# A last chunk finished tile by tile, and four smaller moves in a fused attention and mixture-of-experts kernel

## The chip, the cores and the metric

The kernel runs on one core of one Trainium2 chip. The metric is the time of the whole program on that core in microseconds (us): the median of three runs, 1008.57 us before the change (1008.33 to 1008.92). Lower is better.

## The reference, cut to what matters

x has 4096 rows of 128 values. Eight layers of linear attention with a feed-forward block come first; then a mixture of four experts, of which each row uses the two with the highest router weight. Every step ends in a layer norm.

```
x = _layernorm(x + attn(x))                       # 8 layers: q, k, v; elu; K*v and K summed over rows; Wo, gelu;
                                                  # layer norm; Wf1, gelu, Wf2, gelu; layer norm
h_norm = layer_norm(x, rn_g, rn_b)
g = softmax(h_norm @ router_w.T);  top2_w, top2_idx = top_k(g, 2);  top2_w /= sum(top2_w) + 1e-8
hid = relu(layer_norm(x @ w1[e], ln_g, ln_b));    expert_out[e] = hid @ w2[e]
out = layer_norm(sum of top2_w * expert_out over the two, on_g, on_b)
result = _layernorm(x + out)                      # its own mean and variance, no scale
```

## The kernel before

The kernel is written by hand in five instruction streams, one for each engine: `block.sync` (SyncE, the DMA queue), `block.scalar` (ScalarE), `block.tensor` (TensorE), `block.vector` (VectorE) and `block.gpsimd` (GpSimd). In each stream the order is the order of the calls, and semaphores (`wait_ge`, `then_inc`) tie the streams together. Nothing reorders the work: an instruction that waits holds up all that stands behind it on its engine.

**The layers.** Rows come in 32 units of 128 x 128 halves (`u`, `h`; 512 columns to a half), and `run(step)` walks 33 steps in which one unit is projected (`project`), another attends (`attend`) and a third goes through its feed-forward block (`hidden`, `feed_out`), each some 24 us. Products in the `F32R` format come in three parts, high by high, high by low and low by high (`product`, L823 to L825), so weights and inputs are split into a high and a low half first. `first_step` of the tensor stream begins with `fill(44, mean_r)`: 44 products of constants into the bank `O[1]` (L830), which nobody reads. Then come the first products K, V and Q. Their inputs are `wqkv_l` (L1273) and `xr_l` (L1292) of VectorE, which then adds 1 to the parameters (L1669) and begins on K with `min_k` (L1298), `make_k` (L1305) and `k_by_v` (L1314); ScalarE gives it exponentials (`exp_k`, L465). GpSimd splits inputs 4 and 5 (`low_first`, L1944) and after that, in its steps 0 to 3, the weights of the next layer in four pieces (`split_weights`, L1953, L1956, L1963, L1966). In steps 0 to 2 it waits for nothing but the loaded weights and its own earlier pieces; from step 3 on each piece waits for `xl_done[1]`.

**The experts.** The rows are now worked in 8 chunks of 512 rows, 4 tiles of 128 to a chunk. `run_moe(step)` makes 8 steps; a step (it, k) does three things at once: it begins chunk k+1 (`enters`) and routes chunk k (`routes`), it takes chunk k-1 through the experts (`mixes`), and it ends chunk k-2 (`ends`: both layer norms and the store). The last step, (2, 4), only mixes chunk 8 and ends chunk 7; what remains of chunk 8 stands behind it. Within a step:

- TensorE makes eight expert products (`expert_hidden`, L1047 to L1056) into three banks `R`, with the gram products of the next chunk between them (`gram`, L1085 to L1087, all into the bank `O[0]`), from which VectorE takes the variances (`squares`, L1511). ScalarE empties each `R` bank (`relu`, L584).
- `route` (L1066, L1067) multiplies the chunk by the router's weights, into `O[0]` as well, and so waits for all 16 `squares`. VectorE makes the gates from it (`gates`: 20 small operations from L1548 on, with ScalarE's exponential L623 among them) and splits the standard deviations (`split_std`, L1522 to L1528); TensorE turns these (`turn_std`, L1009, into the bank `SV`) and ScalarE copies them out (`rows_of_std`, L553).
- `expert_out` (L1099) makes the output of one tile, 8 products over the 8 parts of `hid`, into `O[1]` (in the trace Ob) or `CB[0]` (Ca) in turn; `mix_tile` (L1627, L1631) on VectorE adds the four experts by their gates. The order on TensorE is `expert_out` 0, `turn_std`, `expert_out` 1, 2, 3.
- The end of a chunk: `stats_mix` (L1443 to L1463) on VectorE, a power on GpSimd (L2049), `negate_mean` (L1646), `norm_mix` on ScalarE (L594), scale and residual on GpSimd (`scale_and_add`, L2061, L2064, with `add_on_b`, L2070, for the residual), `stats_sum`, the power again, `norm_sum` on ScalarE (L604), and one store.

Behind the last step chunk 8 is ended in two pairs of tiles: `last_moments` (L1879 to L1896) on VectorE, `last_root_of` on ScalarE (a logarithm L808 and an exponential L811), `last_scaled` (L1907, L1913), the same once more for the second norm, and `last_result` (L1922), with one store to a pair (L447).

## Time and profile before

| | |
|---|---|
| median of three runs | 1008.57 us (1008.33 to 1008.92) |
| the profiled execution | 1008.5 us, of which the span from first to last instruction is 1006.7 us |
| TensorE matmul, busy | 954.6 us (95%) |
| VectorE, busy | 888.4 us (88%) |
| ScalarE, busy | 825.6 us (82%) |
| GpSimd, busy | 99.2 us (10%) |
| the layers | 0 to about 824 us |
| one chunk of the experts in the steady part | about 22.35 us |
| the last step and what is behind it | 975.3 to 1006.7 us |

In a row of the timeline the first number is the start in us from the span's beginning, the second the time in us that the row covers; then come the engine (PE is TensorE, PEld its weight loads, DVE VectorE, ACT ScalarE, POOL GpSimd, SPq the DMA queue of SyncE), the line, the operation, what is written and read, and the count. In brackets stand the idle time of the engine just ahead and what ended it. Numbers of buffers are left out, so that `R` is any of three banks. Operations of one engine overlap in the records, so that the distance between two starts tells what one costs the queue.

### The profile page before, as it was taken

The numbers are of one execution on the slowest core, as the hardware profiler recorded it, in microseconds if no ns is written. First come the engines' busy times: TensorE is split into PE (matmuls) and PEld (weight loads), VectorE is DVE, ScalarE is ACT, GpSimd is POOL, SyncE is SP. The second block draws the span as 40 slices with busy tenths as digits, with TensorE's granted clock in tenths as the row PEclk, the third lists the DMA queues.
The fourth block names the chain that finished last, engine by engine and source line by source line (L and its number), as shares of the span: only waits on it lengthen the run. The fifth ranks groups of instructions, "written<-read, shape, count | busy, mean of one in ns | idle before, by whom it ended". The sixth has DMA issues, their size and how long they took to land.

```text
span 1006.7 us, 13398 instructions
## 1 busy us (share of the span) xinstructions
PE 954.6 (95%) x3604; PEld 607.4 (60%) x3604; DVE 888.4 (88%) x2338; ACT 825.6 (82%) x1341; POOL 99.2 (10%) x103
## 2 busy tenths in 40 slices
PE   8799999999999999999999999999999889999984
PEld 7455555555555555565555555555555567777773
DVE  6879999999999999999999999999998788888875
ACT  5889999999999999999899999999998854444442
POOL 2000000000000000000000000000001112333331
PEclk9999999999999999999999999999999999999997
DMA  9000000000000000020000000000001000000000
GB/s 342 1 1 0 1 1 1 0 1 1 0 1 1 1 0 1 1 85 0 1 1 7 0 1 1 1 0 1 1 0 62 23 1 1 11 11 12 12 21 21
DMA packets 8200, 15.86 MB, mean 16 GB/s; under 512 B 960, under 2 KB 5440, under 8 KB 8000
## 3 DMA queue, kind: packets, MB, share of 16 engines
q1 hardware_dynamic: 7696, 14.82, 4.2%
q8 instruction: 31, 0.51, 0.2%
q14 instruction: 41, 0.34, 0.1%
q10 hardware_dynamic: 432, 0.20, 0.1%
HBM read 12.92 MB, written 2.10 MB: 15 GB/s over the span
## 4 chain that ended last, share of the span: by engine, by line
PE 64%; ACT 15%; DVE 10%; issue 10%; POOL 1%; POOLq 0%; DVEq 0%; ACTq 0%
PE Oa L929 11%; PE Ob L929 7%; PE R L823 7%; PE R L825 6%; PE R L824 6%; PE SV L970 4%; ACT L668 4%; PE Ob L884 3%; ACT rs L510 2%; ACT L712 2%; ACT rz L489 2%; PE Ca L949 1%; PE Ca L948 1%; PE Cb L884 1%; PE SV L967 1%
## 5 line engine op out<-in xcount | busy, mean ns | idle before, releaser
L529 ACT ACTIVATE hid<-R,par 128x512 f32<-128x512 f32 x224 | 148.6, 698 | 14.2 <-PE R L825 12.2
L929 PE MATMUL Oa<-hid,wraw 128*128 128x512 f32 x256 | 134.6, 607 | 2.6 <-ACT hid L529 1.1
L929 PE MATMUL Ob<-hid,wraw 128*128 128x512 f32 x256 | 130.8, 592 | 0.0
L823 PE MATMUL R<-x_h,wf_h 128*128 128x512 f32 x224 | 106.1, 474 | 0.5 <-ACT hid L529 0.5
L510 ACT ACTIVATE rs<-SV,eps_ln 128x512 f32<-128x512 f32 x128 | 88.3, 690 | 10.1 <-PE SV L970 5.1
L1358 DVE SCALAR_TENSOR_TENSOR y<-x,par,y 128x512 f32<-128x512 f32 x120 | 87.4, 747 | 3.4 <-ACT y L538 3.1
L823 PE MATMUL R<-xr_h,wqkv_h 128*128 128x512 f32 x156 | 86.8, 556 | 2.5 <-DVE Kt L1314 1.1
L1369 DVE TENSOR_TENSOR y_l<-y,y_h 128x512 fp32r<-128x512 f32 x128 | 87.8, 686 | 1.2
L824 PE MATMUL R<-x_l,wf_h 128*128 128x512 f32 x224 | 88.0, 393 | 0.0
L825 PE MATMUL R<-x_h,wf_l 128*128 128x512 f32 x224 | 87.9, 392 | 0.0
L515 ACT ACTIVATE rs<-rs 128x512 f32<-128x512 f32 x128 | 80.7, 631 | 1.2
L929 PEld LDWEIGHTS Oa<-hid,wraw 128*128 128x128 f32 x256 | 45.9, 189 | 36.4 <-ACT hid L529 27.9
L823 PEld LDWEIGHTS R<-x_h,wf_h 128*128 128x128 f32 x224 | 42.1, 188 | 41.8 <-issue 35.9
L970 PE MATMUL SV<-y,mean_all 128*128 128x512 f32 x128 | 65.6, 594 | 1.6 <-ACT rs L510 0.9
L1345 DVE SCALAR_TENSOR_TENSOR V<-Q,kv,rz 128x512 f32<-128x512 f32 x64 | 46.6, 748 | 23.1 <-ACT rz L494 23.1
L929 PEld LDWEIGHTS Ob<-hid,wraw 128*128 128x128 f32 x256 | 48.2, 189 | 24.5 <-issue 16.3
L1365 DVE CAST y_h<-y 128x512 fp32r<-128x512 f32 x128 | 54.4, 425 | 8.9 <-PE R L949 6.7
L825 PE MATMUL R<-xr_h,wqkv_l 128*128 128x512 f32 x156 | 62.0, 398 | 0.0
L824 PE MATMUL R<-xr_l,wqkv_h 128*128 128x512 f32 x156 | 62.0, 397 | 0.0
L499 ACT ACTIVATE y<-Ca 128x512 f32<-128x512 f32 x65 | 38.7, 595 | 25.2 <-PE Ca L949 25.2
L1314 DVE SCALAR_TENSOR_TENSOR Kt<-R,par,Kt 128x512 f32<-128x512 f32 x62 | 46.3, 746 | 10.9 <-PE R L825 10.5
L604 ACT ACTIVATE reluq<-V,rz 128x128 f32<-128x128 f32 x28 | 11.5, 483 | 52.7 <-DVE rz L1646 44.4
(274 smaller groups left out, 2413.4 us busy)
## 6 DMA issues: line engine op xcount, KB each, us to landing
wraw<-w_dram SPq DMA_DIRECT2D x7, 768.0 KB, 11.9
x<-x_dram SPq DMA_DIRECT2D x8, 256.0 KB, 6.0
Q<-x_dram SPq DMA_DIRECT2D x1, 2048.0 KB, 7.8
out_dram<-reluq SPq DMA_DIRECT2D x7, 256.0 KB, 2.3
wraw<-w_dram SPq DMA_DIRECT2D x2, 512.0 KB, 5.5
wraw<-w_dram SPq DMA_DIRECT2D x1, 576.0 KB, 6.4
wraw<-row_dram SPq DMA_DIRECT2D x1, 512.0 KB, 5.1
wraw<-bias_dram SPq DMA_DIRECT2D x1, 512.0 KB, 6.5
```

The costliest lines, as they stand in the source:

```text
L510: nc.scalar.activation(rs[:, half(h)], SV[:, :], ACT.Ln, bias=eps_ln[:, :]).then_inc(ln_done[which], 1)
L515: nc.scalar.activation(rs[:, half(h)], rs[:, half(h)], ACT.Exp, scale=-0.5).then_inc(rs_done[which], 1)
L529: nc.scalar.activation(hid[:, m * CH:(m + 1) * CH], HIDDEN[m][:, :], GELU, bias=param(u // 4, BF1 + m % FB)).then_inc(hid_done, 1)
L823: nc.tensor.matmul(bank, w_h, a_h, start=True, stop=False)
L824: nc.tensor.matmul(bank, w_h, a_l, start=False, stop=False)
L825: return nc.tensor.matmul(bank, w_l, a_h, start=False, stop=True)
L929: mm = nc.tensor.matmul(O[h][:, :], raw(u // 4, WF2 + j * P, P), hid[:, m * CH:(m + 1) * CH], start=(j == 0), stop=(j == FB - 1))
L970: mm = nc.tensor.matmul(SV[:, :], mean_all[:, :], y[which][:, half(h)], start=True, stop=True)
L1345: nc.vector.scalar_tensor_tensor(out=V[:, half(h)], in0=Q[:, chunk(u, h)], scalar=kv[:, b:b + 1], in1=rz[:, half(h)], op0=ALU.mult, op1=AL ...
L1358: nc.vector.scalar_tensor_tensor(out=g, in0=t, scalar=b, in1=g, op0=ALU.add, op1=ALU.add).then_inc(y_done[which], 1)
L1365: nc.vector.tensor_copy(y_h[:, half(h)], y[which][:, half(h)]).then_inc(yh_done[which], 1)
L1369: nc.vector.tensor_tensor(y_l[:, half(h)], y[which][:, half(h)], y_h[:, half(h)].bitcast(F32), ALU.subtract).then_inc(yl_done[which], 1)
```

## The change

1. **The last chunk by tiles.** Each tile of chunk 8 is ended by itself. The last addition of `mix_tile` also gives the sum of the row (`accum_out`), `end_centre` makes the mean from it, ScalarE's `end_rstd_of` takes the square of the centred tile with its row sum, a logarithm and an exponential, and `end_scaled` does scale and residual, again with a row sum for the second norm. `end_result` is stored tile by tile. The steps of tile t stand between those of tile t+1's mixing.
2. **The chunk ahead of it on VectorE and ScalarE.** Chunk 7 is ended without GpSimd: `chunk7_rstd` on ScalarE takes the place of the powers, `chunk7_scaled` and `chunk7_result` on VectorE that of `norm_mix`, `scale_and_add` and `norm_sum`. VectorE does it ahead of the mixing of chunk 8. ScalarE's `norm_sum` of chunk 6 is moved out of the end of step (2, 3) to between the `relu` of the last step.
3. **Banks in the last step.** Output tile 2 of chunk 8 goes into `O[0]`, and tile 3 into four banks, one for each expert (`last_tile_out`), so that TensorE no longer waits for the mixing; `expert_out` of tile 0 waits for each part of `hid` by itself.
4. **The router in another bank.** From chunk 3 on `route` writes `SV` in place of `O[0]` and waits for no `squares`; `turn_std`, which writes `SV` too, waits for the first gate step.
5. **Deviations turned later.** `turn_std` stands behind `expert_out` of tile 1.
6. **Fewer unread products**: 22 in place of 44. And GpSimd's pieces 0 to 2 of the second layer's weights wait for `xh_done[0]` of steps 1 to 3.

```diff
...
+        def router_bank(n):
+            return O[0] if n <= 2 else L[0]
...
         def mixed_bank(n, t):
+            if (n, t) == (CHUNKS, 2):
+                return O[0]
             return R[2] if n == 1 and t % 2 else MIXED[t % 2]
+        def last_bank(e):
+            return (C, L[0], R[0], R[1])[e]
...
+            sp.wait_ge(chunk7_step, 3 * TILES)
+            sp.dma_start(out[:, (CHUNKS - 2) * TILES:(CHUNKS - 1) * TILES, :],
+                         mix[:, half(0)].rearrange("p (t d) -> p t d", t=TILES)).then_inc(out_stored, 16)
+            for t in range(TILES):
+                sp.wait_ge(end_step[t], 5)
+                sp.dma_start(out[:, (CHUNKS - 1) * TILES + t, :], mix[:, par_tile(1, t)]).then_inc(out_stored, 16)
+            sp.wait_ge(out_stored, 16 * (CHUNKS - 1 + TILES))
...
-                    if ends and m == 4:
+                    if ends and m == 4 and not final:
+                    if final and 2 <= m < 6:
+                        norm_sum_tile(it, 1, m - 2)
+                    if final and m == 2:
+                        chunk7_rstd(MIX)
+                    if final and m == 7:
+                        chunk7_rstd(SUM)
...
-                if ends:
+                if ends and it < 2:
                     norm_sum(it, k - 2)
+            def chunk7_rstd(which):
+                act.wait_ge(var_eps_done[which], CHUNKS - 1)
+                nc.scalar.activation(var_eps[which], var_eps[which], ACT.Ln).then_inc(chunk7_root, 1)
+                act.wait_ge(chunk7_root, 2 * which - 1)
+                nc.scalar.activation(rstd[which], var_eps[which], ACT.Exp, scale=-0.5).then_inc(chunk7_root, 1)
+            def end_rstd_of(t, n):
+                col = slice(t, t + 1)
+                act.wait_ge(end_step[t], (1, 4)[n])
+                nc.scalar.activation(unused[:, tile(t)], mix[:, par_tile(1, t)], ACT.Square,
+                                     bias=end_mean[n][:, col], accum_out=end_var[n][:, col]).then_inc(end_root[t], 1)
+                act.wait_ge(end_root[t], 3 * n + 1)
+                nc.scalar.activation(end_var[n][:, col], end_var[n][:, col], ACT.Ln, bias=moe_eps[:, :],
+                                     scale=1.0 / P).then_inc(end_root[t], 1)
+                act.wait_ge(end_root[t], 3 * n + 2)
+                nc.scalar.activation(end_rstd[n][:, col], end_var[n][:, col], ACT.Exp,
+                                     scale=-0.5).then_inc(end_root[t], 1)
             run_moe(step)
+            act.wait_ge(square_done, CHUNKS * TE)
+            for t in range(TILES):
+                end_rstd_of(t, 0)
+                if t > 0:
+                    end_rstd_of(t - 1, 1)
+            end_rstd_of(TILES - 1, 1)
...
-                elif n == 3:
-                    pe.wait_ge(ln_done[1], 2 * UNITS)
+                else:
+                    pe.wait_ge(gate_step, (n - 1) * GATE_STEPS + 1)
...
-                pe.wait_ge(square_done, 2 * EXPERTS if n == 1 else n * TE)
+                if n <= 2:
+                    pe.wait_ge(square_done, (2, 2 * TILES)[n - 1] * EXPERTS)
+                else:
+                    pe.wait_ge(std_rows_done, n - 1)
+                    if n == 3:
+                        pe.wait_ge(ln_done[1], 2 * UNITS)
-                    both = O[0][:, 2 * t * EXPERTS:2 * (t + 1) * EXPERTS]
+                    both = router_bank(n)[:, 2 * t * EXPERTS:2 * (t + 1) * EXPERTS]
...
-                pe.wait_ge(relu_done, n * HB)
+                if (n, t) != (CHUNKS, 0):
+                    pe.wait_ge(relu_done, n * HB)
...
-                after(pe, mix_done, ((n - 1) * TILES + t - 1) * EXPERTS)
+                if (n, t) == (CHUNKS, 2):
+                    pe.wait_ge(square_done, CHUNKS * TE)
+                    pe.wait_ge(gate_step, (CHUNKS - 1) * GATE_STEPS + 1)
+                else:
+                    after(pe, mix_done, ((n - 1) * TILES + t - 1) * EXPERTS)
                 for m in range(HB):
+                    if (n, t) == (CHUNKS, 0):
+                        pe.wait_ge(relu_done, (n - 1) * HB + m + 1)
                     mm = nc.tensor.matmul(mixed_bank(n, t)[:, tile(m // 2)], hid[:, tile(t, m * CH)], w2[:, tile(m)],
...
+            def last_tile_out():
+                for m in range(HB):
+                    mm = nc.tensor.matmul(last_bank(m // 2)[:, tile(0)], hid[:, tile(TILES - 1, m * CH)], w2[:, tile(m)],
+                                          start=(m % 2 == 0), stop=(m % 2 == 1))
+                    if m % 2 == 1:
+                        mm.then_inc(last_out_mm, 1)
...
-                fill(44, mean_r[:, :])
+                fill(22, mean_r[:, :])
...
                     expert_out(it, k - 1, 0)
+                if mixes:
+                    expert_out(it, k - 1, 1)
                 if routes:
                     turn_std(it, k)
                 if mixes:
-                    expert_out(it, k - 1, 1)
                     expert_out(it, k - 1, 2)
-                    expert_out(it, k - 1, 3)
+                    if (it, k) == (2, 4):
+                        last_tile_out()
+                    else:
+                        expert_out(it, k - 1, 3)
...
+                        total = None
+                        if n == CHUNKS and e == EXPERTS - 1:
+                            total = end_sum[0][:, t:t + 1]
                         nc.vector.scalar_tensor_tensor(out=o, in0=mixed_bank(n, t)[:, tile(e)], scalar=gate[:, c:c + 1],
-                                                       in1=o, op0=ALU.mult, op1=ALU.add).then_inc(mix_done, 1)
+                                                       in1=o, op0=ALU.mult, op1=ALU.add,
+                                                       accum_out=total).then_inc(mix_done, 1)
...
+            def end_centre(t, n):
+                if n == 0:
+                    dve.wait_ge(mix_done, ((CHUNKS - 1) * TILES + t + 1) * EXPERTS)
                 else:
...
+                    dve.wait_ge(end_step[t], 3)
+                nc.vector.tensor_scalar(end_mean[n][:, t:t + 1], end_sum[n][:, t:t + 1], -1.0 / P, None,
+                                        ALU.mult).then_inc(end_step[t], 1)
+            def end_scaled(t):
+                yield
+                o = mix[:, par_tile(1, t)]
+                dve.wait_ge(end_root[t], 1)
+                nc.vector.scalar_tensor_tensor(out=o, in0=o, scalar=end_mean[0][:, t:t + 1], in1=on_g,
+                                               op0=ALU.add, op1=ALU.mult).then_inc(end_step[t], 1)
+                yield
+                dve.wait_ge(end_step[t], 2)
+                dve.wait_ge(end_root[t], 3)
+                nc.vector.scalar_tensor_tensor(out=o, in0=o, scalar=end_rstd[0][:, t:t + 1],
+                                               in1=xb[:, par_tile(1, t)], op0=ALU.mult, op1=ALU.add,
+                                               accum_out=end_sum[1][:, t:t + 1]).then_inc(end_step[t], 1)
+                yield
+                end_centre(t, 1)
+            def end_result(t):
+                o = mix[:, par_tile(1, t)]
+                dve.wait_ge(end_root[t], 6)
+                nc.vector.tensor_scalar(o, o, end_mean[1][:, t:t + 1], end_rstd[1][:, t:t + 1], ALU.add,
+                                        ALU.mult).then_inc(end_step[t], 1)
...
+            def chunk7_scaled():
+                dve.wait_ge(chunk7_root, 2)
...
+            def chunk7_result():
+                dve.wait_ge(chunk7_root, 4)
...
+            def last_step():
+                weave(stats_mix(2, 2))
+                chunk7_scaled()
+                weave(statistics(SUM, 2, 2, mix[:, half(0)]))
+                chunk7_result()
+                weave(mix_tile(2, 3, 0))
+                end_centre(0, 0)
+                weave(mix_tile(2, 3, 1), end_scaled(0))
+                end_centre(1, 0)
+                weave(mix_tile(2, 3, 2), end_scaled(1))
+                end_centre(2, 0)
+                weave(last_tile_mixed(), end_scaled(2))
+                end_centre(3, 0)
+                end_result(0)
+                weave(end_scaled(3))
+                end_result(1)
+                end_result(2)
+                end_result(3)
...
-                if 3 <= s < UNITS - 1:
+                if s < 3:
+                    pool.wait_ge(xh_done[0], upto(s, 0))
+                elif s < UNITS - 1:
```

How the order of TensorE stands around the router, before and with the change (chunk 8's routing; `rw_parts` is the router's weights, `consts` by `wraw` the turning of the deviations, `wraw` by `hid` an output tile):

```order
L1066 MATMUL Oa<-rw_parts,x_h 128x8 [waits square_done,xe_l_done]
L1067 MATMUL Oa<-rw_parts,x_l 128x4
...
L1099 MATMUL Ob<-wraw,hid 128x128 [waits mix_done,relu_done]
L1099 MATMUL Ob<-wraw,hid 128x128 x7
L1009 MATMUL SV<-consts,wraw 36x128 [waits std_rows_done,std_split]
L1009 MATMUL SV<-consts,wraw 36x128 x3
L1099 MATMUL Ca<-wraw,hid 128x128 [waits mix_done,relu_done]
L1099 MATMUL Ca<-wraw,hid 128x128 x7
L1099 MATMUL Ob<-wraw,hid 128x128 [waits mix_done,relu_done]
```

```order
L1108 MATMUL SV<-rw_parts,x_h 128x8 [waits std_rows_done,xe_l_done]
L1109 MATMUL SV<-rw_parts,x_l 128x4
...
L1148 MATMUL Ob<-wraw,hid 128x128 [waits mix_done,relu_done]
L1148 MATMUL Ob<-wraw,hid 128x128 x7
L1148 MATMUL Ca<-wraw,hid 128x128 [waits mix_done,relu_done]
L1148 MATMUL Ca<-wraw,hid 128x128 x7
L1046 MATMUL SV<-consts,wraw 36x128 [waits std_rows_done,gate_step,std_split]
L1046 MATMUL SV<-consts,wraw 36x128 x3
L1148 MATMUL Ob<-wraw,hid 128x128 [waits mix_done,relu_done]
```

The router's products have changed their bank from Oa to SV and no longer wait for `square_done`, and the turning has moved behind the second output tile.

ScalarE in the last step, with the change (`hid` is the `relu`, `reluq` the result of chunk 6, L830 and L832 are chunk 7's logarithm and exponential, L838 to L844 are one pass of `end_rstd_of`):

```order
L599 ACTIVATE hid<-R 128x512 [waits expert_out_mm,expert_mm] x3
L617 ACTIVATE reluq<-V,rz 128x128 [waits out_stored,minus_mean_sum_done,rstd_sum_done]
L830 ACTIVATE rz<-rz 128x4 [waits var_eps_mix_done]
L832 ACTIVATE rz<-rz 128x4 [waits chunk7_root]
L599 ACTIVATE hid<-R 128x512 [waits expert_out_mm,expert_mm]
L617 ACTIVATE reluq<-V,rz 128x128 [waits out_stored,minus_mean_sum_done,rstd_sum_done]
...
L599 ACTIVATE hid<-R 128x512 [waits expert_out_mm,expert_mm] x2
L830 ACTIVATE rz<-rz 128x4 [waits var_eps_sum_done]
L832 ACTIVATE rz<-rz 128x4 [waits chunk7_root]
L838 ACTIVATE Kt,rz<-V,rz 128x128 [waits end0_step,square_done]
L841 ACTIVATE rz<-rz,moe_eps 128x1 [waits end0_root]
L844 ACTIVATE rz<-rz 128x1 [waits end0_root]
```

Before, eight `relu` with chunk 7's `norm_mix` behind the fifth stood here, and `norm_sum` of chunk 6 ahead of them all.

VectorE while it mixes tile 1 of chunk 8, before and with the change:

```order
L1627 TENSOR_SCALAR V<-Ca,rz 128x128 [waits gate_step,expert_out_mm]
L1443 BN_STATS rz<-V 128x6 [waits sum_done]
L1631 SCALAR_TENSOR_TENSOR V<-Ca,rz,V 128x128 [waits mix_done]
L1443 BN_STATS rz<-V 128x6
L1631 SCALAR_TENSOR_TENSOR V<-Ca,rz,V 128x128 [waits mix_done]
```

```order
L1686 TENSOR_SCALAR V<-Ca,rz 128x128 [waits gate_step,expert_out_mm]
L1693 SCALAR_TENSOR_TENSOR V<-Ca,rz,V 128x128 [waits mix_done]
L1967 SCALAR_TENSOR_TENSOR V<-V,rz,wraw 128x128 [waits end0_root,end0_step]
L1693 SCALAR_TENSOR_TENSOR V<-Ca,rz,V 128x128 [waits mix_done]
L1973 SCALAR_TENSOR_TENSOR V,rz<-V,rz,expk 128x128 [waits xb_done,end0_root,end0_step]
L1693 SCALAR_TENSOR_TENSOR V,rz<-Ca,rz,V 128x128 [waits mix_done]
L1957 TENSOR_SCALAR rz<-rz 128x1 [waits end0_step]
```

Before, chunk 7's statistics (BN_STATS) stood between the additions of tile 1; now the two scaling steps of tile 0 (L1967, L1973) stand there, each behind a wait for ScalarE.

## Rows read from the trace of the kernel before

**Rows 1.** The page, part 1: busy us, share of the span and instructions of each engine.

```profile
PE 954.6 (95%) x3604; PEld 607.4 (60%) x3604; DVE 888.4 (88%) x2338; ACT 825.6 (82%) x1341; POOL 99.2 (10%) x103
```

**Rows 2.** The timeline, 1 to 20 us; columns as told above.

```profile
1.25 9.65 PE L830 MATMUL Ob<-mean_r 128*128 128x128 f32 x44 [1.25 <-DVE mean_r L1267]
...
5.48 0.69 DVE L1292 TENSOR_TENSOR xr_l<-x,xr_h 128x512 fp32r<-128x512 f32 x1
...
9.28 0.21 DVE L1669 TENSOR_SCALAR bias<-par 128x104 f32<-128x104 f32 x1
...
10.70 0.73 PE L823 MATMUL R<-xr_h,wqkv_h 128*128 128x512 f32 x1
...
12.82 0.40 PE L825 MATMUL R<-xr_h,wqkv_l 128*128 128x512 f32 x1
...
13.05 0.40 PE L823 MATMUL R<-xr_h,wqkv_h 128*128 128x512 f32 x1
...
13.12 0.43 DVE L1298 TENSOR_SCALAR expk<-expk 128x512 f32<-128x512 f32 x1 [3.64 <-ACT expk L465]
...
19.76 1.09 DVE L1298 TENSOR_SCALAR expk<-expk 128x512 f32<-128x512 f32 x1 [0.48 <-ACT expk L465]
```

**Rows 3.** The timeline, 22 to 26 us.

```profile
22.52 1.00 POOL L1956 TENSOR_TENSOR wqkv_l<-wraw,wqkv_h 128x384 fp32r<-128x384 f32 x1
...
22.68 1.87 DVE L1329 TENSOR_SCALAR expq<-expq 128x512 f32<-128x512 f32 x2
```

**Rows 4.** The timeline of GpSimd, and of VectorE, 86 to 92 us.

```profile
86.55 1.28 POOL L1966 TENSOR_TENSOR wf_l<-wraw,wf_h 128x512 fp32r<-128x512 f32 x1 [62.28 <-DVE xr_l L1414]
...
90.90 0.74 DVE L1414 SCALAR_TENSOR_TENSOR x_l<-x,par,x_h 128x512 fp32r<-128x512 f32 x1
```

**Rows 5.** The timeline, 943 to 951 us, chunk 7's routing.

```profile
943.86 1.26 POOL L2061 TENSOR_TENSOR V<-V,wraw 128x512 f32<-128x512 f32 x1
...
944.15 0.24 PE L1066 MATMUL Oa<-rw_parts,x_h 128*128 128x8 f32 x1 [0.21 <-DVE Kt L1511]
...
945.21 1.27 POOL L2064 TENSOR_TENSOR V<-V,expk 128x512 f32<-128x512 f32 x1
945.21 0.19 DVE L1548 TENSOR_REDUCE rz<-Oa 128x16 f32<-128x32 f32 x1 [1.21 <-PE Oa L1067]
...
945.43 1.07 DVE L1551 TENSOR_TENSOR rz<-rz 128x16 f32<-128x16 f32 x1
...
948.45 0.61 PE L1009 MATMUL SV<-consts,wraw 128*36 128x128 f32 x4 [0.65 <-DVE wraw L1528]
...
950.89 0.35 DVE L1627 TENSOR_SCALAR V<-Ca,rz 128x128 f32<-128x128 f32 x1
```

**Rows 6.** The timeline, 977 to 988 us, the last step.

```profile
977.48 0.87 DVE L1443 BATCH_NORM_STATS2 rz<-V 128x6 f32<-128x128 f32 x4
977.60 1.65 ACT L604 ACTIVATE reluq<-V,rz 128x128 f32<-128x128 f32 x4 [7.35 <-DVE rz L1646]
...
979.45 1.01 POOL L2049 TENSOR_TENSOR rz<-rz,mhalf 128x4 f32<-128x4 f32 x1 [3.75 <-DVE rz L1463]
...
979.78 0.50 PE L1047 MATMUL R<-x_h,xr_h 128*128 128x512 f32 x1 [1.48 <-ACT hid L584]
...
983.97 1.54 ACT L584 ACTIVATE hid<-R 128x512 f32<-128x512 f32 x3
...
987.65 0.35 DVE L1627 TENSOR_SCALAR V<-Ob,rz 128x128 f32<-128x128 f32 x1 [5.92 <-PE Ob L1099]
```

**Rows 7.** The timeline, 995 to 1005 us, behind the last step.

```profile
995.54 0.29 ACT L808 ACTIVATE rz<-rz,moe_eps 128x2 f32<-128x2 f32 x1 [0.16 <-DVE rz L1896]
...
996.11 0.35 DVE L1907 SCALAR_TENSOR_TENSOR V<-V,rz,wraw 128x128 f32<-128x128 f32 x1 [0.34 <-ACT rz L811]
...
1003.86 0.60 DVE L1922 TENSOR_SCALAR reluq<-V,rz 128x128 f32<-128x128 f32 x2 [0.60 <-ACT rz L811]
```

**Rows 8.** The timeline of ScalarE at 812 us.

```profile
812.67 1.28 ACT L755 ACT_TABLE_LOAD   x1
```

151 lines of the change are left out of this document (58 added, 93 removed).

## The prediction

> **What bounds the kernel now.** I read the page first: TensorE is busy 95% of the span, VectorE 88% [rows 1]. TensorE bounds the layers, about 800 us which the change hardly touches. A mean over the span says nothing of the ends, so I went through the timeline at the places of the diff: the start, one boundary between chunks, and the last step with what follows it. In each the question is which wait ends last.
>
> At the start TensorE is busy and does nothing useful: 44 unread products run from 1.25 us, 0.215 us each, until the first real one starts at 10.70, though its last input is begun at 5.48 and written by 6.2 [rows 2]. VectorE has nothing left to do from 9.5 to 13.12 [rows 2]. At a chunk's boundary the chain runs router, gates, mixing of tiles 0 and 1, next chunk's products: TensorE waits for VectorE's squares, then VectorE 1.21 us for the router [rows 5]. In the last step ScalarE holds TensorE up: it does the four results of chunk 6 from 977.60 on, TensorE waits 1.48 us until 979.78, and VectorE sits idle 5.92 us before it mixes at 987.65 [rows 6]. Behind that, the two pairs of tiles pass through VectorE and ScalarE to 1004.46 [rows 7].
>
> **Start: 3.7 us.** With 22 unread products the last ends near 1.25 + 22 x 0.215 = 6.0, so the first real product goes at 6.2, when its input is there, 4.5 us earlier. VectorE can begin on K once its addition to the parameters is over, 9.5 against 13.12: 3.6 us. TensorE's clock decides whether it keeps up. Products of 512 columns start 0.43 us apart at first, the rate of 1.2 GHz, and 0.23 apart from 12.82 to 13.05, that of 2.4 GHz (one lasts 0.73 at 10.70, and 0.40 later) [rows 2]: the clock rose some 2 us after the real products had begun, while 9.4 us of unread ones had left it low. So I take it that the real products raise it, now near 9 us. Then K and V of the second unit are made by 12.5, ahead of VectorE's need. If it stays low until 12.7, 15 products fit in before and TensorE's lead is 2.3 us only.
>
> GpSimd's pieces of weights leave 22 to 24.3 us. There VectorE's two minima took 1.87 us [rows 3]; alone such a one takes 0.43 [rows 2], so about 1.0 us is freed, of which I count half, as ScalarE's exponential of the next K is due at the same time. 3.6 + 0.5 = 4.1. The block of 0.66 at 19.76 (1.09 for 0.43 [rows 2]), by GpSimd's inputs, stays. The pieces land in steps 1 to 3, beside operations that read PSUM or in idle time, with one exception: the fourth piece, which ran in the clear at 86.55, queues behind the third and now runs at about 90.0 to 91.3, over the start of VectorE's low half at 90.90 [rows 4], for which TensorE waits. That costs 0.4. Net 3.7; bounds 1.5 (clock late, nothing from the minima) and 5.5. The layers pass the shift on whole.
>
> **Chunk boundaries: 1.6 us.** The router's products no longer wait for the squares. The row shows 0.21 idle, and a 512-column product is recorded 0.40 long where the next may start after 0.23, so they go 0.37 earlier [rows 2, 5]. But most of this meets GpSimd. VectorE's second gate operation, at 945.43, lasts 1.07 us instead of 0.17, until GpSimd's addition of 945.21 is over [rows 5]. Shifted by 0.37 it would be due at 945.06, at the end of GpSimd's multiplication (943.86 + 1.26), slip in between the two and leave the third operation blocked instead. I count 0.15 for chunks 3 to 7 and the full 0.37 for chunk 8, whose gates are clear of GpSimd.
>
> That rests on rows alone. The Trainium skill (SBUF, "Who interferes with whom") says the same pair of ports serves both engines, that the one which issues first holds it for its whole instruction, and that `tensor_reduce` never contends. The trace agrees (0.19 for the reduction at 945.21, beside GpSimd, against 1.07 for the addition behind it). If GpSimd's second instruction took the pair first each time, the 0.15 would be nothing and the sum 0.75 less.
>
> Turning the deviations later takes 0.65 + 0.45 us (the wait ahead of 948.45, and four small products [rows 5]) out of the way of output tile 1. VectorE begins on that tile at 950.89, right when it is made; by its own queue it could 0.13 earlier. So 0.13 per chunk, six times. ScalarE's copy, for which the next chunk's products wait, comes 1 us later and still 4 us early. Together 5 x 0.15 + 0.37 + 0.78 = 1.9; I take 1.6. Bounds: 0 and 6 x (0.37 + 0.13) = 3.0.
>
> **Last step and end: 5.8 us.** ScalarE loses the four scalings of `norm_mix`; those of `norm_sum` (four in 1.65, about 0.40 apart [rows 6]) move between the `relu`, which frees TensorE of its 1.48. Chunk 7 on VectorE: statistics end at 979.45, logarithm and exponential give the root 0.57 later (995.54 to 996.11) [rows 6, 7], so 980.0; eight scalings 0.26 apart (two of this size in 0.60, the first 0.34 [rows 7]) to 982.2; the statistics again, 1.97 (977.48 to 979.45), to 984.2. ScalarE meanwhile makes from 980.0 on five `relu` at 0.55 (three in 1.54 [rows 6]) and three results at 0.42, to 984.1; then the root, to 984.85; VectorE's four results end at 985.95. TensorE has tile 0 by 984.5 and never waits again. So the mixing starts at 985.95 where it started at 987.65 [rows 6]. It is VectorE that gates it now, with chunk 7's work.
>
> Tile 0 takes four dependent additions (0.35 and the hand-over, 0.39 each) and the mean, which reaches ScalarE at 987.75. ScalarE then makes eight passes: a square of 128 columns (0.40, as a result), the read of its row sum, then logarithm and exponential (0.57 until VectorE has it [rows 7]). The row sum on ScalarE is in no row: I bound it by nothing and by a small ScalarE operation with its hand-over, 0.29 [rows 7] and some 0.06, and take 0.15, about midway, so 1.1 to 1.2 a pass and 9.5 for eight. About 0.9 goes in waits for VectorE, whose additions alternate with steps that wait for ScalarE. So 998.2, the last result done at 998.7 against 1004.46: 5.8 earlier. GpSimd does nothing meanwhile, and the single tile's store leaves as before. Bounds: a row sum of 0.35 (8 x 0.20 = 1.6 later) and one of nothing (8 x 0.15 = 1.2, and 0.2 of the waits, earlier).
>
> A rule speaks against it: the Trainium skill (Vector Engine (DVE) Microarchitecture Reference, "Points that are easy to get wrong") has it that this kind of operation with two fp32 sources in SBUF halves its rate when the accumulator is read. That is the second scaling of each tile. No row shows such a one with its sum. By the rule each would take about 0.13 more and the sum would lose up to 0.5.
>
> **Sum.** 1008.5 (profiled: span 1006.7 and 1.8 around it) - 3.7 - 1.6 - 5.8 = 997.4. The median, 1008.57, stands 0.1 above the profiled time: 997.4.
>
> **The rivals.**
> - *The start gives little* (0.14). The clock stays low until 12.7 as now, and ScalarE's exponentials come late. For it: nothing shows the clock with fewer unread products. Against: 9.4 us of them left it low. The start gives 1.0: 1000.1.
> - *ScalarE's passes are longer* (0.14). Each costs 0.35 more and VectorE's alternating additions are held with them: 8 x 0.35 = 2.8, 1000.2.
> - *More than I count* (0.08). Row sum free, gates clear of GpSimd, minima whole: 994.5.
> - *The bank and the turning do nothing* (0.04). The gates end where GpSimd does: 999.0.
> - *Slower* (0.02). Squares, logarithms and exponentials alternate 16 times; if each change loaded a table, at 1.28 us [rows 8], 20.5 us would come on top: 1017.9. It decides from 9 loads on (11.1 / 1.28). Against: the order with the change shows no load there, and squares in the layers follow logarithms without one.
> - Several together (0.02) bring it within 2 us of before.
>
> **How the numbers follow.** The forecast itself has 0.56. Start 1.5 to 5.5, boundaries 0 to 3.0, end 4.2 to 7.2 sum to 992.8 to 1002.8; not all fall one way at once, and the first two rivals lie inside, so 993.5 to 1002.0. A measurement of this kernel tells 0.2%, 2 us, from no change. Faster by more 0.96, within it 0.02, slower 0.02.
>
> **What would show it.** The first real product at 6.2 and K's minimum at 9.5; the low half of the third unit held near 90; the router directly behind the last expert product, with another gate operation of 1.07 us; tile 1 made before the turning; the first mixing of the last step near 975 + 11, less the shift; eight ScalarE passes of 1.2; the last result 5.8 earlier relative to the last step's first product. It is wrong if the shift at the first K is under 2 us or lost in the layers, if ScalarE's pass exceeds 1.5 us, or if VectorE's chunk 7 work holds the mixing beyond where it started before.

## The result and the profile after

The changed kernel takes 992.38 us (median of four runs, 990.87 to 993.93) against 1008.75 us in the same comparison (1008.33 to 1009.28): ratio 0.9843, 95% interval 0.9829 to 0.9856. It gained 16.4 us where 11.2 were forecast, and lies below the range. One execution of the kernel before, beside e1 to e4, took 1334.07 us at a granted clock of 0.656 where all others have 0.986 to 0.997; the ratios leave it out.

The profiled execution is the slowest of the four, 993.93 us with a span of 992.1. So the traces have 14.6 us to explain; the other 1.8 lie in the differences between runs, which e4 and e8 take up. Times in the table are us, and the mixing of output tile 1 is the one in the step that routes chunk 8.

| stage of the profiled executions | before | after | gain | forecast |
|---|---|---|---|---|
| start, up to the deviations of chunk 1 (L1522, now L1581) | 814.55 | 811.81 | 2.74 | 3.7 |
| from there to the mixing of output tile 1, chunk 8's routing | 156.90 | 153.18 | 3.72 | 1.6 |
| from there to the first product of the last step | 3.86 | 3.85 | 0 | 0 |
| from that product to the first mixing | 12.34 | 10.23 | 2.11 | 1.7 |
| from the mixing to the end of the last result | 16.81 | 11.12 | 5.69 | 4.1 |
| from there to the end of the span | 2.23 | 1.94 | 0.29 | 0 |

The page of the changed kernel, part 1, answers to [rows 1]:

```profile
PE 948.7 (96%) x3582; PEld 604.7 (61%) x3582; DVE 887.5 (89%) x2332; ACT 828.9 (84%) x1361; POOL 94.7 (10%) x99
```

**The start.** Its timeline, beside [rows 2]:

```profile
1.25 4.96 PE L866 MATMUL Ob<-mean_r 128*128 128x128 f32 x22 [1.25 <-DVE mean_r L1327]
...
6.00 0.76 PE L859 MATMUL R<-xr_h,wqkv_h 128*128 128x512 f32 x1
...
9.64 0.69 DVE L1352 TENSOR_TENSOR xr_l<-x,xr_h 128x512 fp32r<-128x512 f32 x1 [0.83 <-ACT xr_h L647]
9.91 0.40 PE L859 MATMUL SV<-xr_h,wqkv_h 128*128 128x512 f32 x1
...
10.25 0.21 DVE L1732 TENSOR_SCALAR bias<-par 128x104 f32<-128x104 f32 x1
...
10.50 0.43 DVE L1358 TENSOR_SCALAR expk<-expk 128x512 f32<-128x512 f32 x1
```

The first real product is 4.7 us earlier, and a product of 512 columns lasts 0.40 from 9.91 on: the clock has risen some 3 us earlier than before. That is read from the products alone; the granted clock of the profile is 1.00 up to 20 us in both traces. But K's minimum starts at 10.50, not at 9.5. The last input's low half is begun at 9.64 here, since its transfer came later, and before at 8.67:

```profile
8.67 0.69 DVE L1292 TENSOR_TENSOR xr_l<-x,xr_h 128x512 fp32r<-128x512 f32 x1 [0.57 <-ACT xr_h L630]
```

In all fourteen traces with 22 unread products (the change and e1, e4 to e15) the minimum starts 0.85 or 0.86 us behind that low half, at 9.34 to 11.11, and at 10.1 in the mean. In the three with 44 (before, e2, e3) it starts at 13.12 or 13.13, also where the low half began at 9.80 (e3). So the shorter start lets the arrival of the last input count.

**The boundaries.** The timeline at the gates of chunk 6, and of chunk 7, beside [rows 5] (L1610, L1614, L1618 and L1621 are the second to the fifth gate operation, L2162 is GpSimd's addition):

```profile
918.17 0.17 DVE L1610 TENSOR_TENSOR rz<-rz 128x16 f32<-128x16 f32 x1
...
918.38 1.27 POOL L2162 TENSOR_TENSOR V<-V,expk 128x512 f32<-128x512 f32 x1
918.38 1.29 DVE L1614 TENSOR_TENSOR rz<-rz,prep_small 128x16 f32<-128x16 f32 x1
...
940.69 0.17 DVE L1614 TENSOR_TENSOR rz<-rz,prep_small 128x16 f32<-128x16 f32 x1
940.70 1.30 POOL L2162 TENSOR_TENSOR V<-V,expk 128x512 f32<-128x512 f32 x1
...
940.90 0.17 DVE L1618 TENSOR_REDUCE rz<-rz 128x4 f32<-128x16 f32 x1
...
941.10 0.93 DVE L1621 TENSOR_TENSOR rz<-rz 128x16 f32<-128x16 f32 x1
```

In chunk 6 the third operation meets GpSimd's addition and is held until it ends, as forecast. In chunk 7 VectorE is 0.01 us ahead: the third passes, the fourth (a reduction) passes beside GpSimd, and only the fifth is held. So two operations fewer are left when GpSimd ends. Chunk 3 goes as chunk 7, chunks 4 and 5 as chunk 6. Measured at the mixing of tile 1 the six boundaries of chunks 3 to 8 give 0.74, 0.35, 0.36, 0.35, 0.75 and 1.20 us.

Chunk 8, before and then after:

```profile
971.45 0.35 DVE L1627 TENSOR_SCALAR V<-Ca,rz 128x128 f32<-128x128 f32 x1 [0.66 <-PE Ca L1099]
```

```profile
964.50 0.60 PE L1046 MATMUL SV<-consts,wraw 128*36 128x128 f32 x4
...
964.99 0.34 DVE L1686 TENSOR_SCALAR V<-Ca,rz 128x128 f32<-128x128 f32 x1
```

VectorE had stood idle 0.66 us for output tile 1. With the turning behind that tile it does not wait.

**The end.** The last step and two passes of ScalarE, beside [rows 6, 7] (L2004 is chunk 7's result, L838 a square, then the read of its row sum, L841 the logarithm, L844 the exponential, L1967 and L1973 VectorE's scalings, L1982 a result):

```profile
968.84 0.48 PE L1084 MATMUL R<-x_h,xr_h 128*128 128x512 f32 x1
...
978.04 1.12 DVE L2004 TENSOR_SCALAR V<-V,rz 128x128 f32<-128x128 f32 x4 [0.51 <-ACT rz L832]
979.07 0.35 DVE L1686 TENSOR_SCALAR V<-Ob,rz 128x128 f32<-128x128 f32 x1
...
982.87 0.40 ACT L838 ACTIVATE Kt<-V,rz 128x128 f32<-128x128 f32 x1 [0.94 <-DVE rz L1957]
...
983.17 0.18 ACT L838 ACTIVATION_READ_ACCUMULATOR Kt<-V,rz 128x1 f32 x1
983.39 0.29 ACT L841 ACTIVATE rz<-rz,moe_eps 128x1 f32<-128x1 f32 x1
983.46 0.35 DVE L1967 SCALAR_TENSOR_TENSOR V<-V,rz,wraw 128x128 f32<-128x128 f32 x1
983.72 0.20 ACT L844 ACTIVATE rz<-rz 128x1 f32<-128x1 f32 x1
...
983.83 0.39 ACT L838 ACTIVATE Kt<-V,rz 128x128 f32<-128x128 f32 x1
984.01 0.35 DVE L1973 SCALAR_TENSOR_TENSOR V<-V,rz,expk 128x128 f32<-128x128 f32 x1
...
989.85 0.34 DVE L1982 TENSOR_SCALAR V<-V,rz 128x128 f32<-128x128 f32 x1 [0.60 <-ACT rz L844]
```

VectorE gates the mixing with chunk 7's results, as forecast. From 982.87 on ScalarE's squares follow at 0.94 to 1.03 us, and the profile shows no wait between them: that chain sets the end. No table load stands among them.

### The profile page after: what moved, and what is told of

It reads as the page before. It is cut to its first block, busy times and chain, and to the rows that moved or that the text cites. A ratio compares the mean times of both kernels' runs of the same rounds, so it can differ in the third digit from the quotient of the medians.

```text
span 992.1 us, 13389 instructions
## 1 busy us (share of the span) xinstructions
PE 948.7 (96%) x3582; PEld 604.7 (61%) x3582; DVE 887.5 (89%) x2332; ACT 828.9 (84%) x1361; POOL 94.7 (10%) x99
## 4 chain that ended last, share of the span: by engine, by line
PE 59%; ACT 20%; DVE 10%; issue 10%; DMA 1%; SPq 0%; ACTq 0%; DVEq 0%
PE Oa L965 12%; PE R L859 6%; PE Ob L965 6%; PE R L861 5%; PE R L860 5%; ACT L685 4%; PE SV L1006 4%; ACT rs L525 3%; PE Ob L920 3%; ACT L729 3%; ACT rz L504 2%; ACT hid L544 2%; DVE V L1693 2%; PE Ca L985 1%; ACT expq L487 1%
## 5 line engine op out<-in xcount | busy, mean ns | idle before, releaser
L859 PEld LDWEIGHTS R<-xr_h,wqkv_h 128*128 128x128 f32 x156 | 30.0, 192 | 42.5 <-DVE xr_l L1474 27.9
```

Of the source, the lines that this page charges most:

```text
L859: nc.tensor.matmul(bank, w_h, a_h, start=True, stop=False)
```

## The experiments

All comparisons are with the kernel before on the same chip, five rounds each. "Period" is the distance between the routers of two chunks. Stage times are those of the profiled execution: gates of chunk 2 to tile 1 of chunk 8 (before 137.89 us, after 134.14), last step's first product to the mixing, mixing to the last result's end.

**Which part gives what (e1 to e4).** The diffs are parts of the change: e1 has the start alone,

```diff
-                fill(44, mean_r[:, :])
+                fill(22, mean_r[:, :])
...
-                if 3 <= s < UNITS - 1:
+                if s < 3:
+                    pool.wait_ge(xh_done[0], upto(s, 0))
+                elif s < UNITS - 1:
```

e2 has `router_bank` with its waits and `turn_std` behind `expert_out` 1, e3 all the rest, e4 is the whole.

> The kernel before with the start alone changed: 22 unread products in place of 44, and GpSimd's three pieces of weights held for their steps. The trace with the whole change shows 2.6 to 2.8 us gained by 51 us and kept through the layers, with one stretch at 1.2 GHz more (34 to 37 us) than before. Theory A (the start is worth what that trace shows): 1006.0 us in the profiled run, a boundary of chunks still 22.35 us. Rival B (the extra slow stretch is a matter of the single run and costs some 1.6 us where it falls): runs without it at about 1004.3, so that the runs lie 1.5 to 2 us apart. Rival C (forecast): 3.7 us, 1004.8.

> The kernel before with the router's other bank and the later turning alone, start and end as before. Theory A (each boundary gains as in the trace of the whole change: 0.74, 0.35, 0.36, 0.35, 0.75 and 1.20 us at chunks 3 to 8): 3.7 us less, 1005.0, and the period of a chunk 22.0 in place of 22.35. Rival B (chunks 3 and 7 gained 0.4 more there since VectorE's third gate operation started 0.01 us ahead of GpSimd's addition, which is a matter of phase): 2.9 us less, 1005.8, with the third operation blocked in chunks 3 and 7. Rival C (forecast): 1.6 to 1.9 us, 1006.9.

> The changed kernel with start, router's bank and turning put back: the last chunk by tiles, chunk 7 on VectorE and ScalarE, and the banks of the last step. Theory A (trace of the whole change: mixing 10.2 us behind the first product of the last step in place of 12.3, and 11.1 us from there to the last result in place of 16.8): 7.8 us less, 1001.0. Rival C (forecast): 5.8 us, 1003.0. ScalarE's passes should be 1.0 us apart (A) or 1.15 (C).

> The changed kernel once more, unedited. Its four runs lay 3.1 us apart (990.9 to 993.9) where the kernel before has 1 us. Theory A: the number of stretches at 1.2 GHz differs from run to run, so that time and mean granted clock go together: some 1.6 us for each 0.0017 of the clock. Rival B: the times differ at an equal clock, by the arrival of the first inputs. The profiled run falls anywhere between 990.5 and 994.

| | median us (runs) | ratio, 95% | less than before |
|---|---|---|---|
| e1 | 1003.01 (1002.26 to 1004.12) | 0.9950, 0.9937 to 0.9962 | 5.3 |
| e2 | 1004.62 (1003.95 to 1006.0) | 0.9964, 0.9951 to 0.9977 | 3.7 |
| e3 | 1000.28 (999.55 to 1002.08) | 0.9922, 0.9909 to 0.9935 | 8.0 |
| e4 | 992.24 (991.03 to 992.97) | 0.9844, 0.9830 to 0.9858 | 16.0 |

The parts sum to 17.0, the whole gives 16.0: nearly additive. The end's 8.0 and the boundaries' 3.7 agree with the traces; the start is worth more than the profiled execution of the change shows, and e1 came out below all three of its expectations, of which 1004.3 was the lowest. In e4 the runs do not go in order with the mean clock (992.92 at 0.990, 991.03 at 0.992, 992.24 at 0.994), so theory A of e4 fell in that form: the mean also counts low clock behind the last product (0.5 from 984.5 on in e4's trace). The traces show another source of spread. Of the five boundaries of chunks 3 to 7 VectorE's third gate operation came ahead of GpSimd's addition in none in e14 (stage 134.91), in one in e2 and e8 (134.55 and 134.61), in two in the change and e10 (134.14 and 134.10) and in three in e4 (133.73): 0.4 us for each, and a different number in each execution. The third operation starts 0.43 to 0.44 behind the first every time, and the addition 0.41 to 0.45 (in one of e4's three it is recorded 0.005 ahead, and VectorE passes all the same). Theory A of e2 is right in the sum, and rival B in that the 0.4 is a matter of phase.

**Turning and bank apart (e5, e6).** e5 is the changed kernel with `turn_std` back between `expert_out` 0 and 1, e6 with `route` back in `O[0]` behind its squares.

> The changed kernel (992.3 us) with the deviations turned between output tiles 0 and 1 again, the router's bank kept. Theory A: turning ahead of tile 1 costs 0.13 us in chunks 3 to 7 and 0.66 to 0.74 in chunk 8, where VectorE has no low half of the next chunk to make and stood idle for 0.66 us: 1.4 us more, 993.7. Rival C (forecast): 0.13 in each of six, 0.8 us more, 993.1. TensorE would wait for VectorE's first gate operation and the split ahead of the turning.

> The changed kernel with the router in its old bank, behind the squares, the later turning kept. Theory A: what is left of the 3.7 us at the boundaries when the turning's 1.4 is off, 2.3 us, comes from the bank: 994.6, and no gate operation behind VectorE's second is blocked by GpSimd. Rival C (forecast): 0.15 in five chunks and 0.37 in the sixth, 1.1 us more, 993.4.

e5: 994.15 us (992.94 to 994.84), ratio 0.9854, 0.9837 to 0.9870; the stage takes 135.68. e6: 994.73 (993.36 to 996.92), ratio 0.9862, 0.9844 to 0.9881; the stage takes 136.44, and the second gate operation is held again, for 1.07 or 1.08 in chunks 3 to 7. In e5 VectorE's third operation comes first in two chunks, as in the change and e10, and against these (134.14 and 134.10) the turning is worth 1.5 us: 0.13 to 0.16 in each of chunks 3 to 7 and 0.78 in chunk 8. The bank is worth 2.3 against them. Against e14, in which the third operation never comes first, it is 1.5; the rest is the 0.4 for each chunk in which it does. Both come out as theory A has them, twice the forecast.

**Who holds whom at a boundary (e7, e13).** One wait more in GpSimd's `scale_and_add`, for n up to 5:

```diff
+                if n <= CHUNKS - 3:
+                    pool.wait_ge(std_split, 3 * (n + 2))                 # e7
+                    pool.wait_ge(gate_step, (n + 1) * GATE_STEPS + 3)    # e13, instead
                 nc.gpsimd.tensor_tensor(o, o, xb[:, half(k % 2)], ALU.add).then_inc(sum_done, 1)
```

> The changed kernel with one wait more: in the steps that route chunks 3 to 7, GpSimd's addition of the residual waits until VectorE has split the deviations. Theory A (at a boundary VectorE's gates are held by GpSimd's addition until it ends, 0.9 to 1.3 us): no gate operation over 0.2 us, gates 0.7 to 1.1 us earlier, the addition holds a later operation for 0.4, and TensorE's wait ahead of output tile 2 (0.61 us in chunk 6, 0.23 in chunks 3 and 7) goes: 2.3 us less, 990.0. Rival B (the boundary is bound by the length of the gates' chain, GpSimd only overlaps it, or the addition holds up as much where it is put): 992 or more.

> The changed kernel with one wait more: in the steps that route chunks 3 to 7 GpSimd's addition waits for VectorE's third gate operation. Theory A (in the traces so far a chunk takes 21.60 us where VectorE's third gate operation was issued ahead of that addition, and 21.98 where it came second; which of them wins differs from chunk to chunk by 0.01 us): VectorE ahead in all five chunks, period 21.6 to 21.7, 0.4 us less in each chunk that is lost otherwise, about 1 us in all, 991.3, and the gates' fifth operation held in place of the third. Rival B (the order is not what decides): periods still mixed between 21.6 and 22.0, 992.3.

e7: 990.79 us (990.29 to 991.18), ratio 0.9821, 0.9806 to 0.9836. e13: 991.72 (991.44 to 992.36), ratio 0.9837, 0.9823 to 0.9850. The timeline of e7 in chunk 6 (L2164 is the addition, L1639 a gate operation on two SBUF sources), then of e13:

```profile
917.72 0.17 DVE L1587 TENSOR_TENSOR wraw<-rz,std_h 128x16 f32<-128x16 f32 x1
...
918.05 1.27 POOL L2164 TENSOR_TENSOR V<-V,expk 128x512 f32<-128x512 f32 x1 [2.40 <-DVE wraw L1587]
...
918.66 0.88 DVE L1639 TENSOR_TENSOR rz<-rz 128x64 f32<-128x64 f32 x2
```

```profile
915.19 0.19 DVE L1607 TENSOR_REDUCE rz<-SV 128x16 f32<-128x32 f32 x1 [0.78 <-PE SV L1109]
...
915.97 1.27 POOL L2164 TENSOR_TENSOR V<-V,expk 128x512 f32<-128x512 f32 x1 [0.44 <-DVE rz L1614]
916.04 1.23 DVE L1621 TENSOR_TENSOR rz<-rz 128x16 f32<-128x16 f32 x1
```

In e7 no gate operation is held; the addition runs mostly beside operations that read PSUM (L1560, L1686), which it does not hold, and then lengthens L1639's pair from 0.35 to 0.88. The periods from chunk 3 to 6 are 21.69 and the stage takes 133.50. That is 0.8 less than the mean of the five traces whose boundaries are as in the change (134.30, with e4, e8, e10 and e14), and the median is 17.8 below that of the kernel before where e4's is 16.0; theory A had 2.3. It was right on the hold and too high on what would be left. In e13 the order was forced as meant, but the period was 21.9 and the stage took 134.55. My expectation failed: the addition now waits for the third operation and starts 0.78 us behind the first (915.97 against 915.19) where it had started 0.41 to 0.45 behind, and that eats what the order gives. What counts is when the addition ends and how many operations are then left; who comes first is one way to change that.

**The row sum on ScalarE (e14).**

```diff
-  ... ACT.Square, bias=end_mean[n][:, col], accum_out=end_var[n][:, col])
-  nc.scalar.activation(end_var[n][:, col], end_var[n][:, col], ACT.Ln, ...
+  ... ACT.Square, bias=end_mean[n][:, col])
+  nc.scalar.activation(end_var[n][:, col], moe_eps[:, :], ACT.Ln, ...
```

> The changed kernel without the row sums of ScalarE's eight squares; the logarithm takes a constant, so that the roots of the last chunk are left out of the result. It prices the row sum, which the forecast took at 0.15 us, within 0 to 0.35. A pass now takes 1.0 us. Theory A (the read of the row sum, recorded 0.19, begins before the square's end and holds the queue 0.12): passes of 0.87, at least where ScalarE sets the pace, the last four: 0.5 to 1.0 us less behind the start of the mixing, 991.5. Rival B (the read is hidden in the hand-over to the logarithm): passes of 1.0, 992.3.

e14: 991.65 us (989.71 to 993.82), ratio 0.9838, 0.9823 to 0.9852, too wide to price it; the trace does. One pass:

```profile
983.27 0.39 ACT L838 ACTIVATE Kt<-V,rz 128x128 f32<-128x128 f32 x1
983.69 0.29 ACT L841 ACTIVATE rz<-moe_eps 128x1 f32<-128x1 f32 x1
984.02 0.20 ACT L844 ACTIVATE rz<-rz 128x1 f32<-128x1 f32 x1
```

From square to logarithm it takes 0.42 where the change took 0.52: the row sum costs the queue 0.10. Mixing to last result takes 10.63 in place of 11.12, 0.5 in all. Theory A.

**Chunk 7's results away from VectorE (e10).** `chunk7_result` becomes four `nc.gpsimd.tensor_scalar` at GpSimd's end.

> The changed kernel with chunk 7's four results on GpSimd, idle there, in place of VectorE. Theory A (VectorE's work on chunk 7 sets the start of the mixing: the four results take 1.12 us from 978.0 and output tile 0 is ready at 978.2): mixing 0.8 us earlier and all behind it, 991.5. GpSimd's operations run while VectorE reads PSUM and hold nothing up. Rival B (the eight passes of ScalarE set the end, and the mixing has slack): 992.3. Rival C (GpSimd holds up VectorE's scaling): 992.3 or more.

e10: 990.64 us (990.12 to 992.56), ratio 0.9823, 0.9809 to 0.9836. Its timeline (L2197 is the new place of chunk 7's results):

```profile
977.52 0.35 DVE L1686 TENSOR_SCALAR V<-Ob,rz 128x128 f32<-128x128 f32 x1 [0.68 <-PE Ob L1148]
977.53 3.15 POOL L2197 TENSOR_SCALAR V<-V,rz 128x128 f32<-128x128 f32 x4 [7.72 <-ACT rz L832]
...
979.96 0.51 DVE L1967 SCALAR_TENSOR_TENSOR V<-V,rz,wraw 128x128 f32<-128x128 f32 x1
```

The mixing starts 9.37 us behind the last step's first product, not 10.23, and now waits for TensorE. Behind it 11.30 in place of 11.12: GpSimd took 0.79 an operation, ran into VectorE's first scaling (0.51 for 0.35) and took some 0.17 back. Net 0.7 by the trace, theory A but for its "hold nothing up"; the median fell by more (18.3 below the kernel before where e4 has 16.0).

**What the start is made of (e9).** The kernel before with `fill(22)` alone.

> The kernel before with 22 unread products in place of 44 and nothing else. With GpSimd's waits as well it gained 5.3 us (1003.0). Theory A (GpSimd's pieces of weights beside VectorE's two minima at 22 us are worth what the forecast freed there, 0.5 to 1.0 us): 1003.8, the pair of minima still 1.1 us longer than in that run. Rival B (with the start moved the pieces fall beside other work, and the waits give nothing): 1003.0.

e9: 1004.91 us (1003.29 to 1005.67), ratio 0.9957, 0.9945 to 0.9970; 4.0 less, where e1 has 5.3. The two minima with GpSimd's pieces beside them, and then in e1 without:

```profile
18.84 1.01 POOL L1956 TENSOR_TENSOR wqkv_l<-wraw,wqkv_h 128x384 fp32r<-128x384 f32 x1
...
18.99 1.89 DVE L1329 TENSOR_SCALAR expq<-expq 128x512 f32<-128x512 f32 x2
```

```profile
18.75 0.75 DVE L1329 TENSOR_SCALAR expq<-expq 128x512 f32<-128x512 f32 x2
```

1.14 us come free, and the attention's first V (L1345) is 1.37 earlier (24.74 and 23.37): nothing of it is lost to ScalarE. Theory A.

**The slow stretches (e8).** In the fourteen traces of kernels without the products added below TensorE falls to 1.2 GHz one to three times between 20 and 50 us, for 3.4 us or twice that. e8 gives TensorE unread products in idle time:

```diff
-                fill(14, wqkv_h[0][:, :])
+                fill(19, wqkv_h[0][:, :])
...
+                fill(2, wqkv_h[0][:, :], SV)
                 centre(0, 0, 0)
+                fill(4, wqkv_h[0][:, :], SV)
                 centre(0, 0, 1)
```

> The changed kernel with 5 unread products more behind the first 14 and 6 more (2 and 4) ahead of the two centring products of the first step, in idle time of TensorE at 23 to 31 us. Theory A (the stretches of 3.4 us at 1.2 GHz between 20 and 50 us come after TensorE had stood idle in part, and cost up to 2 us each): one stretch fewer on average, 1 to 2 us less, and runs closer together. Rival B (the stretches come whatever TensorE does there, as they differ from run to run with the same program): 992.3 and the same spread. Each filler may cost 0.1 to 0.3 us where TensorE is waited for.

> The changed kernel with GpSimd's addition behind the gates, chunk 7's results on GpSimd, the unread products at 23 to 31 us, and 5 more in the 32nd step (757 us), where the run with fillers had its only stretch at 1.2 GHz. Theory A (a stretch comes where TensorE has stood idle and can be kept away): no stretch between 20 and 800 us, 1.5 + 0.8 + 1.5 us less than 992.3, that is 988.5, and runs within 0.5 us. Rival B (the stretch moves on to another place): 989.5 to 990.

> The same without any unread products beyond the 22 and 14 of the changed kernel: GpSimd's addition behind the gates and chunk 7's results on GpSimd. Theory A: the two add up, 992.3 - 1.5 - 0.8 = 990.0, runs up to 2 us apart by where the stretches at 1.2 GHz fall. Rival B (one hides the other): 990.8.

> The fastest version so far (chunk 7's results on GpSimd, unread products at 23 to 31 us and at 757 us, median 989.4) with GpSimd's addition behind the third gate operation instead of behind all gates. Theory A (a held gate operation costs 0.37 us less than one held first, and an addition behind the gates gives 0.3 back later): period 21.6 against 21.69, 0.3 us less, 989.1. Rival B: the same, 989.4. Runs with a stretch at 1.2 GHz between 20 and 800 us are slower by up to 2 us each, as before.

| | median us (runs) | ratio, 95% |
|---|---|---|
| e8 | 992.46 (992.42 to 992.62) | 0.9838, 0.9824 to 0.9853 |
| e11 | 989.37 (988.21 to 992.25) | 0.9814, 0.9798 to 0.9830 |
| e12 | 990.60 (989.9 to 990.86) | 0.9818, 0.9805 to 0.9831 |
| e15 | 991.35 (990.96 to 992.75) | 0.9835, 0.9821 to 0.9848 |

Windows of TensorE in the changed kernel, and in e11; the number ahead of the DMA share is the granted clock, 1.00 being 2.4 GHz:

```profile
20.00:24.00 4.00, 4.00 (x14) 0.57 1.01 415
33.00:38.00 5.00, 3.89 (x9) 0.66 0.00 0
43.00:48.00 5.00, 3.88 (x7) 0.66 0.00 0
```

```profile
20.00:24.00 4.00, 4.00 (x23) 1.00 1.00 412
33.00:38.00 5.00, 3.37 (x13) 1.00 0.00 0
43.00:48.00 5.00, 4.82 (x18) 1.00 0.00 0
```

And in e8, then in e9, which has no fillers:

```profile
758.00:763.00 5.00, 4.28 (x9) 0.66 0.00 0
```

```profile
760.00:765.00 5.00, 5.00 (x11) 0.66 0.01 3
```

With the fillers the early stretches are gone in e8, e11 and e15, and e8's four runs lie within 0.2 us. But e8 has one at 759 us, where it loses 1.7 us against e4's trace, and the median stayed. With five more unread products there (e11, e15) chunk 1's deviations are ready at 808.6 and 808.3, where the eleven traces with the short start and no fillers have 809.5 to 811.9. Then e15 has a stretch at 809, and its second chunk routes 17.82 us behind the first in place of 16.33. So theory A holds for the places filled. Rival B, that a stretch moves on to another gap, is not shown: e9 has one at 761 without any filler (1.0 us lost there against e1's trace), and between 812 and 818 the traces of before, the change, e1, e4 and e9 have one. By the traces the fillers at both places are worth 2.0 us at chunk 1's deviations (810.5, the mean of the eleven, against 808.5). e11 is the fastest median, 989.4; its interval overlaps e12's, and one of its five runs took 992.25, so the fillers' own gain of some 1.2 us in the median is not shown. That e11 and e12 beat the change (0.9814 and 0.9818 of before, against 0.9843 and 0.9844) is by e7's and e10's mechanisms, which their stages repeat (133.41 and 133.45; 9.34 and 9.35). e12's median lies between its two theories, and these stages speak for A. e15 had expected 0.3 less than e11 and got 2 more: e13's order costs 1.1 at the boundaries, the stretch 1.5.

## Why the prediction was wrong

The direction, the chance of faster (0.96) and the places were right. The size was 5 us short, and three terms failed to one side. Two of them measured beyond their own upper bounds, 3.7 against 3.0 at the boundaries and 7.8 against 7.2 at the end, so that the result lies below even the 992.8 of all bounds together. "More than I count" had 0.08 and ended at 994.5, still above the result.

**Start, 3.7 forecast.** The profiled execution has 2.7, but with the last input 1 us late and three slow stretches between 20 and 50 us. By e1 it is 5.3; by the traces 4.5, from 815.0 (mean of 814.6, 816.1 and 814.3 in before, e2 and e3) to 810.5 (mean of the eleven above). The step "9.5 against 13.12: 3.6 us" held where the last input came as in the trace before: 9.54 in e1. In the mean of the fourteen traces with 22 unread products it is 3.0, since the arrival of that input was in no term. "Of which I count half" failed: all of it came free, 1.1 us. In e1's trace VectorE is 3.9 us ahead of the kernel before at 20 us, 5.0 at 30 and 4.4 at 51, behind the slow stretches. "That costs 0.4" failed: the fourth piece ran at 87.41 to 88.69 and stretched the low half at 88.31 to 0.92 from 0.75, and nothing was lost behind it (in the change 2.6 earlier at 51 us, 2.7 at 735). The first rival, a clock that stays low until 12.7, is out: products of 512 columns last 0.40 from some point between 8.2 and 11.5 on in these fourteen traces, and the start of K's minimum did not follow it (9.34 in e6 at 11.1, 11.11 in e12 at 8.2). That the clock falls again later, a differing number of times, was in no term.

**Boundaries, 1.6 forecast, 3.7 measured.** Two steps failed. "So 0.13 per chunk, six times" carried chunk 7's queue over to chunk 8. There VectorE has no low half of a next chunk (L1501, 0.68) to make, it stood idle 0.66, and the turning gave 0.78 by e5, 1.5 in all. "I count 0.15 for chunks 3 to 7" was right in kind: the second operation slipped in and the third was held. But what is saved is the whole time of each operation that slips in, 0.21, plus the 0.13 of the turning, which makes the 0.35 of chunks 4 to 6. In chunks 3 and 7 the third slipped in too, and the reduction behind it, for another 0.4 each. I had named that reduction as never held and did not follow it. By e6 the bank is worth 2.3 in place of 1.1.

The Trainium skill (SBUF, "Who interferes with whom") has it that the first to issue holds the pair of ports for its whole instruction, and that reductions don't contend. This trace agrees to 0.01 us (940.69 against 940.70; 0.17 for the reduction at 940.90), and what the prediction set against it, GpSimd's second instruction ahead of VectorE's second operation each time, did not occur in any trace with the new bank.

**Last step and end, 5.8 forecast, 7.8 measured.** The mixing starts 10.23 us behind the first product where 10.64 were worked out (0.4; 0.25 of it are chunk 7's two roots, 0.48 and 0.47 us until VectorE goes on where 0.55 and 0.65 stood). The rest is the step "1.1 to 1.2 a pass and 9.5 for eight": without their waits the eight passes took 8.0. I put logarithm and exponential at 0.57, which is the time until VectorE has the root; ScalarE's own queue is held 0.33 + 0.11 (983.39 to 983.72 to 983.83). That 0.13 counts in the six passes that another follows at once, 0.8 us. Square and row sum, taken at 0.55, take 0.52, another 0.2 in eight; the row sum itself costs 0.10 (e14) where 0.15 stood. And the terms as I had them, 0.40 + 0.15 + 0.57, make 9.0 for eight: 0.5 of the 9.5 stood on no row. First mean at ScalarE 1.80 behind the mixing and 0.94 of waits (both 1.8 and 0.9 in the forecast) held. The rival of longer passes is out, and so is that of table loads. The single tile's store ends 0.3 earlier than the pair's.

The rule that spoke against the change, the Trainium skill (Vector Engine (DVE) Microarchitecture Reference, "Points that are easy to get wrong"), is not borne out: L1973 with its row sum is recorded 0.35 as L1967 without one, and VectorE's next operation starts 0.28 behind it against 0.27 (984.29 against 984.01, 983.73 against 983.46). The measurement decides: nothing for the half rate.

## What to carry to other kernels

Price a chain on one engine by the distance between the starts of its instructions, and a hand-over by the time until the other engine has it; where a queue alternates between several tiles, the first is what it costs. Where two engines exclude one another, follow each instruction until the holder ends, chunk by chunk and with what is missing in the last one: what is left behind the holder is the cost, and 0.01 us may decide it. Before taking a term from one trace, ask how that stage varies between runs; the first 50 us varied here by 2 us, by the arrival of one input and by the clock.

## What the hardware showed that was not expected

- The granted clock fell for about 3.4 us at a time, in places that differed between executions of one program, and cost from 0.4 (e4, 16.78 in place of 16.33 us from the first chunk to the second) to 1.7 us (e8 at 759). Between 20 and 50 us fourteen traces without added unread products have one to three falls, and three with them none.
- A GpSimd addition of 1.27 us held VectorE's `tensor_tensor` on two SBUF sources, and not a reduction or operations that read PSUM. A GpSimd `tensor_scalar` beside VectorE's `scalar_tensor_tensor` on two SBUF sources lengthened it from 0.35 to 0.51 (e10). Which of the two engines came first turned on 0.02 us: the addition won where it started 0.41 to 0.43 behind the first gate operation, and lost where it started 0.43 to 0.45 behind.
- Two 128x128 `tensor_scalar` of VectorE start 0.26 apart (L2004 in the change); the same on GpSimd 0.78 (e10).
